# Fourth layer of a fused attention network: key diagonals placed in four transfers with channels interleaved, and a reordered end

## What is computed

```
x = h + softmax(q k^T / sqrt(128)) v,   h = groupnorm(x)             # layer 0, one head of 128 channels
x = gamma * softmax(q k^T) v + x        # layer 1: attention along rows of the image (16 keys), 16 channels for q, k
x = gamma * softmax(q k^T) v + x        # layer 2: one head over 256 positions, 16 channels for q, k
# layer 3, the fourth: 8 heads of 16 channels, keys and values from the image pooled 3x3 with stride 2
q = x w_q + b_q;  xp = avg_pool(x);  k = xp w_k + b_k;  v = xp w_v + b_v
q, k, v = (a.reshape(batch * 8, positions, 16) for a in (q, k, v))
out = softmax(q k^T / sqrt(16)) v;   x = (out reshaped back) w_o + b_o + x
```

## Time and profile before

| | |
|---|---|
| median of 3 runs | 133.29 us |
| the profiled execution's own time | 132.69 us |
| span of its instructions | 130.8 us |
| busy: TensorE, VectorE, ScalarE, GpSimd | 112.2, 84.2, 76.4, 66.1 us |
| mean granted TensorE clock | 0.961 |
| shares of the chain that ended last | PE 57%, DVE 28%, POOL 4%, DMA 4% |
| DMA | 15521 packets, 6.43 MB |

### The profile page before, as it was taken

One profiled execution on the slowest core, in us unless ns is written; L12 is line 12 of the kernel. 1 busy time (PEld: TensorE's weight loads), 2 busy tenths in 40 slices (PEclk: granted clock), 3 DMA queues, 4 the chain that ended last, 5 costly groups with the idle time before them and its releaser, 6 DMA issues.

```text
span 130.8 us, 3857 instructions
## 1 busy us (share of the span) xinstructions
PE 112.2 (86%) x1510; PEld 84.7 (65%) x1510; DVE 84.2 (64%) x196; ACT 76.4 (58%) x228; POOL 66.1 (51%) x118
## 2 busy tenths in 40 slices
PE   6887999999999999999989997954589668667990
PEld 4565999998777777767668885441345445555890
DVE  5867657645224355588878722869699999970081
ACT  0446267788974656749796735153516565598620
POOL 8302626999810321330038888813264668869700
PEclk9998699999999999999999999999855999999999
DMA  3960000000000000000000033433474550000046
GB/s 86 330 194 0 0 5 0 3 3 3 0 5 0 5 0 0 5 0 0 0 0 0 7 116 85 129 94 83 102 108 116 91 57 5 0 5 5 5 137 184
DMA packets 15521, 6.43 MB, mean 49 GB/s; under 512 B 9360, under 2 KB 14864, under 8 KB 15504
## 3 DMA queue, kind: packets, MB, share of 16 engines
q1 hardware_dynamic: 13744, 4.66, 15.5%
q10 hardware_dynamic: 1760, 1.53, 4.2%
HBM read 4.61 MB, written 1.57 MB: 47 GB/s over the span
## 4 chain that ended last, share of the span: by engine, by line
PE 57%; DVE 28%; POOL 4%; DMA 4%; issue 2%; ACT 2%; POOLq 1%; ACTq 0%; DVEq 0%
PE bank L769 11%; PE bank L714 9%; DVE prob L607 8%; DVE negmax L605 7%; DVE inv L614 6%; PE bank L733 5%; PE bank L753 5%; DMA x_all<-in_x_dram 4%; PE bank L698 4%; PE bank L766 3%; POOL prob L368 3%; PE bank L705 3%; PE bank L835 3%; PE bank L743 2%; PE bank L780 2%
## 5 line engine op out<-in xcount | busy, mean ns | idle before, releaser
L429 ACT ACTIVATE prob<-bank,negmax 128x256 f32<-128x256 f32 (+1 forms) x48 | 19.3, 409 | 13.8 <-DVE negmax L567 10.1
L368 POOL TENSOR_TENSOR prob<-prob,inv 128x512 f32<-128x512 f32 x16 | 16.3, 1042 | 14.3 <-DVE inv L617 14.3
L485 ACT ACTIVATE prob<-prob 128x512 f32<-128x512 f32 x16 | 10.1, 631 | 17.9 <-DVE prob L607 17.9
L769 PE MATMUL bank<-probT,v 128*128 128x256 f32 x64 | 17.0, 388 | 0.4 <-issue 0.4
L714 PE MATMUL bank<-packed,xT 128*128 128x128 f32 (+1 forms) x96 | 16.0, 292 | 0.2 <-ACT prob L429 0.2
L595 DVE SCALAR_TENSOR_TENSOR xT<-bank,packed,xT 128x256 f32<-128x256 f32 x16 | 7.7, 484 | 12.6 <-PE bank L769 7.8
L804 PE MATMUL bank<-packed,prob 128*128 128x128 f32 x64 | 10.9, 302 | 5.4 <-POOL prob L368 3.5
L714 PEld LDWEIGHTS bank<-packed,xT 128*128 128x128 f32 x96 | 13.6, 197 | 2.1 <-issue 1.2
L794 PE MATMUL bank<-kdiag,qT 64*32 64x256 f32 x256 | 10.5, 444 | 5.2 <-ACT probT L489 1.8
L359 POOL TENSOR_TENSOR probT<-turned,packed 128x256 f32<-128x256 f32 x8 | 4.9, 612 | 17.8 <-DVE turned L589 17.8
L769 PEld LDWEIGHTS bank<-probT,v 128*128 128x128 f32 x64 | 11.1, 190 | 3.4 <-issue 2.4
(11 more groups left out here) (102 smaller groups left out, 233.4 us busy)
## 6 DMA issues: line engine op xcount, KB each, us to landing
kdiag<-k_rows SPq DMA_DIRECT2D x28, 64.0 KB, 2.3
out_dram<-x_all SPq DMA_DIRECT2D x8, 128.0 KB, 2.0
x_all<-in_x_dram SPq DMA_DIRECT2D x2, 256.0 KB, 4.1
x_all<-in_x_dram ACTq DMA_DIRECT2D x2, 256.0 KB, 5.4
vdiag<-v_rows SPq DMA_DIRECT2D x8, 64.0 KB, 3.0
packed<-in_pack_dram ACTq DMA_DIRECT2D x1, 321.0 KB, 5.7
k_rows<-kT SPq DMA_DIRECT2D x4, 64.0 KB, 1.8
kdiag<-k_rows ACTq DMA_DIRECT2D x4, 64.0 KB, 2.9
```

The lines of the kernel that those rows point to most:

```text
L368: nc.gpsimd.tensor_tensor(p, p, inv[g][:, t, :].unsqueeze(2).broadcast_to([128, HEADS, KEYS]), ALU.mult)\
L429: last = nc.scalar.activation(prob[g][:, t, 0:keys], psum("scores", layer, g)[:, keys * t:keys * t + keys], ACT.Exp, bias=negmax[g][:, t, ...
L485: nc.scalar.activation(prob[g][:, t, :], prob[g][:, t, :], ACT.Exp).then_inc(s_exp3, 1)
L769: last = mm(ps[:, 0:TOK], vals[:, k, 0:C], probT[g][:, 0, TOK * k:TOK * k + TOK], start=k == 0, stop=k == TILES - 1)
```

## The change

Channels of the fourth layer's queries are ordered on the host (`by_half`) so that partition 64h + 4e + c is channel e of chunk 4h + c: channels outside, chunks inside, within each half of 64 rows. Partitions c, c + 4, ..., c + 124 then hold chunk c of both halves, and one transfer places 32 rows of 4 KB; its source is the block of 16 key rows, read once for each half. Four such transfers of 128 KB replace eight of 64 KB for each pair; for pair 0 two are issued by SP and two by ScalarE's queue.

The end: b_o goes into xT already with the update of layer 2, and its effect on queries, keys and values is taken out of their biases by three small products (`bias`, placed before qk of layer 2) and four small VectorE instructions (the first `biases3` of the diff is VectorE's, of which bq3's line is shown; the second is TensorE's). So `xb` goes, and `x` (transposes and ScalarE's copy) comes early, one place after q. y comes two places after pv instead of eight. The last image's scaling is done by VectorE (`share_last`), and VectorE takes both maxima of an image before both subtractions. Waits on the fourth layer's weights move to the bias step.

```diff
+    def by_half(a):
+        return a.reshape(*a.shape[:-1], HALVES, HCHUNKS, DH).swapaxes(-1, -2).reshape(a.shape)
...
-        {"w3q": i["L3_conv_w_q"], "w3k": by_channel(i["L3_conv_w_k"]), "w3v": i["L3_conv_w_v"], "w3o": i["L3_conv_w_o"],
+        {"w3q": by_half(i["L3_conv_w_q"]), "w3k": by_channel(i["L3_conv_w_k"]), "w3v": i["L3_conv_w_v"], "w3o": i["L3_conv_w_o"],
...
-        steps += [("pool", 3, 1), ("q", 3, 3), ("kv", 3, 0), ("scores3", 3, 5), ("share3", 3, 2), ("probT3", 3, 2),
-                  ("xb", 3, 1), ("pv", 3, 1), ("x", 3, 2), ("y", 3, 6)]
+        steps += [("pool", 3, 1), ("q", 3, 3), ("kv", 3, 0), ("x", 3, 1), ("scores3", 3, 4), ("share3", 3, 2), ("probT3", 3, 2),
+                  ("pv", 3, 1), ("y", 3, 2)]
...
+        sequence.insert(sequence.index(("qk", 2, 0)), ("bias", 3, 0))
...
-        SHARED = HEADS // 2
+        SHARED = HCHUNKS // 2
         def place_chunk(eng, i, c):
-            to = kdiag[i % KEY_BUFFERS][DH * c:DH * c + DH, c % HCHUNKS, :, :]
-            eng.dma_start(to.rearrange("e m n -> e (m n)"), k_dram[i]).then_inc(s_keys[i], 16)
+            to = kdiag[i % KEY_BUFFERS][c:C - HCHUNKS + c + 1:HCHUNKS, c, :, :]
+            rows = k_dram[i].unsqueeze(0).broadcast_to([HALVES, DH, HEADS * PAIR * PTOK])
+            eng.dma_start(to.rearrange("e m n -> e (m n)"), rows).then_inc(s_keys[i], 16)
...
-                for c in range(SHARED if i == 0 else HEADS):
+                for c in range(SHARED if i == 0 else HCHUNKS):
                     place_chunk(sp, i, c)
...
-                if step == "share3":
+                if step == "share3" and g < IMAGES - 1:
...
-                if step == "xb":
-                    wait_filled(pool, "scores1", 3, g)
-                    nc.gpsimd.tensor_scalar(xb[g], xT[g][:, :], part["bo3"], None, ALU.add).then_inc(s_xb, 1)
...
-                        for c in range(SHARED, HEADS):
+                        for c in range(SHARED, HCHUNKS):
                             place_chunk(act, 0, c)
...
+            def biases3():
+                wait_filled(dve, "bias", 3)
+                dve.wait_ge(s_packed[W3], 16)
+                ps = psum("bias", 3)
+                nc.vector.scalar_tensor_tensor(out=part["bq3"], in0=ps[:, C:C + 1], scalar=-1.0, in1=part["bq3"],
+                                               op0=ALU.mult, op1=ALU.add).then_inc(s_bias3, 1)
...
+                nc.vector.scalar_tensor_tensor(out=xT[g][:, :], in0=ps, scalar=part[("bv0", "bv1", "bo3")[layer]],
+                                               in1=xT[g][:, :], op0=ALU.add, op1=ALU.add).then_inc(*drained_by("o", layer, g))
...
+                for h in range(HALVES):
+                    wait_filled(dve, f"scores{h}", 3, g)
+                    nc.vector.tensor_reduce(out=negmax[g][:, h, :], in_=banks[h], op=ALU.max, axis=AX.X, negate=True).then_inc(s_max3, 1)
+                for h in range(HALVES):
+                    dve.wait_ge(s_max3, HALVES * g + h + 1)
+                    nc.vector.tensor_tensor(view(prob[g][:, h, :], HEADS), banks[h],
+                                            negmax[g][:, h, :].unsqueeze(2).broadcast_to([128, HEADS, KEYS]), ALU.add)\
+                        .then_inc(*drained_by(f"scores{h}", 3, g))
...
+            def share_last(g):
+                dve.wait_ge(s_inv3, 2 * (g + 1))
+                for h in range(HALVES):
+                    p = view(prob[g][:, h, :], HEADS)
+                    nc.vector.tensor_tensor(p, p, inv[g][:, h, :].unsqueeze(2).broadcast_to([128, HEADS, KEYS]), ALU.mult)\
+                        .then_inc(s_share_last, 1)
...
-                pe.wait_ge(s_keys[i], 16 * HEADS)
+                pe.wait_ge(s_keys[i], 16 * HCHUNKS)
...
+            def biases3():
+                pe.wait_ge(s_packed[W3], 16)
+                ps = begin("bias", 3)
+                mm(ps[:, 0:C], part["bo3"].broadcast_to([C, 128]), part["w3v"], start=True, stop=True)
+                mm(ps[:, C:C + 1], part["w3q"], part["bo3"], start=True, stop=True)
+                mm(ps[:, C + 1:C + 2], part["w3k"], part["bo3"], start=True, stop=True).then_inc(*filled_by("bias", 3))
...
-                pe.wait_ge(s_xb, g + 1)
+                image_ready(3, g)
```

More of the change, by code:

```diff
@@ L137, in build @@
         poolW = [prob[g][:, 0, 0:SIDE * PSIDE].rearrange("p (h w) -> p h w", w=PSIDE) for g in range(IMAGES)]
-        oT, y, xb = [qT[g][:, 0, :] for g in range(IMAGES)], x_in, [qT[g][:, 1, :] for g in range(IMAGES)]
+        oT, y = [qT[g][:, 0, :] for g in range(IMAGES)], x_in
         bank = [ctx.enter_context(nc.psum_tensor(f"bank{b}", [128, 512], f32)) for b in range(BANKS)]
@@ L168, in build @@
         parts_of = {"scores3": ("scores0", "scores1"), "probT3": ("probT0", "probT1"),
-                    "norm": (), "scale": (), "turn": (), "pool": (), "setup": (), "xb": (), "share3": ()}
+                    "norm": (), "scale": (), "turn": (), "pool": (), "setup": (), "share3": ()}
         for step, layer, g in sequence:
@@ L214, in build @@
         s_max, s_inv, s_scaled = (sem(n) for n in ("max_ready", "inv_ready", "prob_scaled"))
-        s_pool, s_xb = sem("pool_step"), sem("output_bias_added")
+        s_pool, s_bias3 = sem("pool_step"), sem("output_bias_taken_out")
         s_key_rows = sem("key_channels_ready")
@@ L218, in build @@
         s_keys, s_vals = ([sem(f"{n}_placed{i}") for i in range(IMAGES // PAIR)] for n in ("keys", "values"))
-        s_max3, s_exp3, s_inv3, s_share3 = (sem(n) for n in (
-            "max3_ready", "exp3_ready", "inv3_step", "prob3_scaled"))
+        s_max3, s_exp3, s_inv3, s_share3, s_share_last = (sem(n) for n in (
+            "max3_ready", "exp3_ready", "inv3_step", "prob3_scaled", "prob3_scaled_by_vector"))
         v_at = packs[W0][1]["w0v"][0]
@@ L470, in _ @@
                     if g == 0:
-                        act.wait_ge(s_packed[W3], 16)
+                        act.wait_ge(s_bias3, 4)
                     keys3(g)
@@ L474, in _ @@
                     if g == 0:
-                        act.wait_ge(s_bias, 2)
+                        act.wait_ge(s_bias3, 4)
                     queries3(g)
@@ L547, in prepare @@
                 nc.vector.tensor_scalar(part["bv1"], part["bv1"], part["gamma1"], None, ALU.mult).then_inc(s_bias, 1)
-                nc.vector.tensor_scalar(part["bq3"], part["bq3"], float(DH) ** -0.5, None, ALU.mult).then_inc(s_bias, 1)
-                dve.wait_ge(s_bias, 2)
+                dve.wait_ge(s_bias, 1)
+            def biases3():
[4 more added lines that the diff above has]
+                                               op0=ALU.mult, op1=ALU.add).then_inc(s_bias3, 1)
+                nc.vector.scalar_tensor_tensor(out=part["bk3"], in0=ps[:, C + 1:C + 2], scalar=-1.0, in1=part["bk3"],
+                                               op0=ALU.mult, op1=ALU.add).then_inc(s_bias3, 1)
+                nc.vector.scalar_tensor_tensor(out=part["bv3"], in0=ps[:, 0:C], scalar=-1.0, in1=part["bv3"],
+                                               op0=ALU.mult, op1=ALU.add).then_inc(*drained_by("bias", 3))
+                dve.wait_ge(s_bias3, 1)
+                nc.vector.tensor_scalar(part["bq3"], part["bq3"], float(DH) ** -0.5, None, ALU.mult).then_inc(s_bias3, 2)
             def queries_keys0(g):
@@ L593, in update, with scores3 @@
                 ps = psum("o", layer, g)[:, 0:TOK]
[L594 to L609, removed]
+                nc.vector.scalar_tensor_tensor(out=xT[g][:, :], in0=ps, scalar=part[("bv0", "bv1", "bo3")[layer]],
+                                               in1=xT[g][:, :], op0=ALU.add, op1=ALU.add).then_inc(*drained_by("o", layer, g))
+            def scores3(g):
+                banks = [view(psum(f"scores{h}", 3, g)[:, :], HEADS) for h in range(HALVES)]
+                for h in range(HALVES):
[6 more added lines that the diff above has]
+                        .then_inc(*drained_by(f"scores{h}", 3, g))
             def sums3(g):
@@ L640, in _ @@
                     prepare()
+                if step == "bias":
+                    biases3()
                 if step == "scores" and layer == 0:
@@ L652, in _ @@
                     if g == 0:
-                        dve.wait_ge(s_packed[W3], 16)
+                        wait_drained(dve, "bias", 3)
                     wait_filled(dve, "kv", 3, g)
@@ L658, in _ @@
                 if step == "scores3":
-                    for t in range(TILES):
-                        scores3(g, t)
+                    scores3(g)
                 if step == "share3":
                     sums3(g)
+                    if g == IMAGES - 1:
+                        share_last(g)
                 if step == "y":
@@ L800, in turn_prob3 @@
             def turn_prob3(g, t):
-                pe.wait_ge(s_share3, TILES * g + t + 1)
+                if g < IMAGES - 1:
+                    pe.wait_ge(s_share3, TILES * g + t + 1)
+                else:
+                    pe.wait_ge(s_share_last, t + 1)
```

(8 more changed lines are left out.)

2 lines of the change are left out of this document (1 added, 1 removed).

## The result

The changed kernel takes 157.48 us in the median of four runs (156.65 to 159.26), the kernel before 133.95 in runs on the same chip. The ratio is **1.176**, interval [1.162, 1.191]. The profiled execution took 157.12 us, with a span of 155.3.

A forecast was written before the change was run, and what follows sets the result against it. Before: TensorE to 80.4 us, VectorE to 115.7, then the end; keys off the chain. With two engines serving keys, span 151.4 (last reciprocal 142.8, end 8.6) plus 1.9 gives 153.3 us; range 128.5 to 160.

The forecast's parts named there:

- Engines: Key transfers: the doubled source's outermost step counts 2, so two DMA engines serve each, one copy of 64 KB apiece; chance 0.70.
- Price and chain: Key placing: 0.165 us per 4 KB piece, 12.4 us per pair; the chain waits on keys, last reciprocal at 142.8.
- the fixed part: Key transfers' landing: the store's 2.0 us less 0.2, so 1.8 us, besides the pieces.
- the 0.6 for the bias products: TensorE, ahead of the fourth layer: three added products cost 0.6 us, putting pair 0's key issue at 76.94.
- step (d): Before pair 3's key rows SP issues value transfers, 1.4 us, a second couple 0.4; pair 3 issued 116.4, lands 129.2.
- The end: From last reciprocal to the kernel's end: 8.6 us instead of 13.7, a gain of 5.1.
- term (h): The new end after the last reciprocal at 142.8: 8.6 us, giving a span of 151.4.
- The third rival: Two engines, but cold TensorE and late y products eat the end's gain: 13.7 again, 158 us; inside the range.
- The first rival: Key transfers get sixteen engines after all, keys land at about 80 as now: about 130.0 us; chance 0.23.
- Its side remark: Key transfers: eight engines would keep keys ahead of VectorE; four, 7.1 us a pair against 8, only just.
- The second rival: Key transfers on two engines, but pieces at 0.23 us, 14.9 for 10.6 a pair: about 170 us; chance 0.07.
- What was costed at nothing: Layer 2's fused update (0.06 more each, covered; 0.5 if bare), VectorE's four small instructions, host channel order: 0.

## Why the prediction was right, step by step

**Engines.** Right in its mechanism and in its choice: two, by completions, by the DMA share, and by the experiments with 16 or 32, 4 and 2 as the outermost count. The rule that the prediction cites from the Trainium skill (DMA: Bandwidth & Descriptors, "Why a DMA increments its semaphore by 16 and not by 1") agrees with all of them: 16, 4 and 2 completions a transfer.

**Price and chain.** The piece was put at 0.165 us and took 0.164. The steps, forecast and measured:

| | forecast | measured |
|---|---|---|
| pair 0's scores begin | 89.3 | 89.36 |
| pair 1 | 102.0 | 102.23 |
| pair 2 | 114.7 | 115.52 |
| pair 3 | 129.2 | 130.91 |
| last reciprocal | 142.8 | 143.55 |
| end of the span | 151.4 | 155.3 |

A pair was to take 12.4 us from its first issue; it took 13.5, 12.8, 13.1 and 13.9 (75.85 to 89.36, and so on), so with 64 pieces at 0.164 the rest, the fixed part, was 2.3 to 3.4 instead of 1.8 (pair 3's has value pieces in it, which the prediction put at 0.4). The 1.8 came from the store's 2.0 as the best landing; the earlier trace rows has a better one, 1.8 for the key rows, so the term was read from the wrong row, and the right one would have been further off. In pair 0 this was hidden by an issue put 1.1 us too late (76.94 for 75.85; the 0.6 for the bias products does not show before it in this trace): two errors that cancelled, which was luck. At pair 3, step (d), SP itself was held: two value issues took 7.11 us and the key rows' issue 3.23, where the prediction had them waiting in the queue only. It cost little against the forecast: the keys of pair 3 were issued at 117.02 for 116.4, and 0.8 of lateness was there already at pair 2.

**The end** was the step that failed, by size: term (h), 8.6 us, measured 11.75. That is 3.15 of the 3.9 us by which the span was off (155.3 for 151.4); the other 0.75 was there at the last reciprocal. The prediction followed images 6 and 7 alone from the last reciprocal on. TensorE was further behind: pv of image 5 began at 144.78, after that reciprocal, because each pv waits for a copy whose transposes stand just before it. The step list of the kernel before had pv two places after probT3, one of them xb's; taking xb out left one place, and the prediction counts nothing for that. With pv one place later again the term is 9.8 to 10.1. So -5.1 for the end was -2.0 in the span's tail, and in the time no gain is shown (1.176 beside 1.190 for the keys alone). The third rival, an end of 13.7 with 158 us, named the late y products and a cold clock. It came near the time, not the mechanism: the granted clock was 1.00 from 143.5 us to the end, and the chain went over the ring.

**The first rival**, sixteen engines at 130.0, did not occur. Its time was too low as well: where the experiments gave the changed kernel sixteen engines it took 133.3 and 132.1, no change against before that can be told. Its side remark, that four engines would be "only just" enough, held for pairs 1 and 2 and not for the kernel: 1.067, for pair 0, which nothing covers, and for SP, held at pair 3. What it says of eight engines was not run. **The second rival**, pieces at 0.23 and about 170 us, is out: 0.164.

**What was costed at nothing** (the update's fused form, VectorE's small instructions, the host's order of channels) is contradicted by no run. What the x transposes and the bias products cost TensorE was not measured by itself.

## What to carry to other kernels

Before joining transfers, write down the outermost count at both ends and ask how many engines it gives; a block read twice can be written twice instead, which cost nothing that can be told here (132.1 us); putting the repeat inside instead of outermost was not run. If few engines hold a transfer, all that is behind it in the same queue waits as well, and so may the issuing engine. When a step list is shortened, ask for each pair of steps whether another engine's copy lies between: one place too few made a ring of 2.6 us an image, and the place given back took the kernel with rows written twice from 132.11 to 128.35 us.

## What the runs showed of the hardware that was not expected

**Issues that block.** Two value transfers took SP 1.35 us to issue before, and 7.11 us while two engines had the keys of pair 2 before them; later four took 12.26 us. So many 64-byte pieces (1024 a transfer) behind a backlog held the issuing engine, not just the queue. The backlog alone doesn't do it: the key rows' write of 128 pieces took 0.32 us to issue behind the keys of pair 0 (79.42) and 3.23 behind the values (111.85). How many pieces it takes was not measured. SP's timeline of the kernel before and of the changed one:

```profile
92.56 1.35 SPq L290 DMA_DIRECT2D vdiag<-v_rows  x2
...
102.21 2.73 SPq L290 DMA_DIRECT2D vdiag<-v_rows  x4
```

```profile
120.24 12.26 SPq L295 DMA_DIRECT2D vdiag<-v_rows  x4
```

**Issues dearer in part.** With 16 partitions four apart, SP's four issues of pair 0 took 2.74 us, with neighbouring ones in the kernel before 1.73; the eight of pair 1 took 5.89 against 3.54. Those of pair 2 show no difference, 4.91 against 4.97, so the layout alone doesn't set the price. Why was not tried. The lines of pairs 1 and 2 in the kernel with eight transfers, and those of before:

```profile
81.78 5.89 SPq L265 DMA_DIRECT2D kdiag<-k_rows  x8
...
89.61 4.91 SPq L265 DMA_DIRECT2D kdiag<-k_rows  x8
```

```profile
81.18 3.54 SPq L259 DMA_DIRECT2D kdiag<-k_rows  x8
...
87.55 4.97 SPq L259 DMA_DIRECT2D kdiag<-k_rows  x8
```
